# Two attention layers: the value products of two steps in one batch, and 16 buffers of exponentials instead of 8

## The reference

```python
# layer 0: 16 heads of 16, causal
scores = jnp.einsum('bhqd,bhkd->bhqk', q, k) * scale
scores = jnp.where(causal, jnp.finfo(scores.dtype).min, scores)
out = jnp.einsum('bhqk,bhkd->bhqd', jax.nn.softmax(scores, axis=-1), v)
# layer 1: 16 heads, each with two halves of 8 and one v of 16, no mask
def attend(qh, kh):
    scores = jnp.einsum('bthd,bshd->bhts', qh, kh) * SCALE
    p = jax.nn.softmax(scores, axis=-1)
    return jnp.einsum('bhts,bshe->bthe', p, v12)
a = attend(q1, k1) - lam * attend(q2, k2)     # then a norm and Wo
```

## Time and profile before

| | us |
|---|---|
| median of 3 runs | 4248.61 |
| lowest, highest | 4227.96, 4248.86 |
| profiled execution, its own time | 4232.43 |
| its span | 4230.7 |
| granted TensorE clock, mean | 0.894 |

### The profile page before, as it was taken

The page is one execution under the profiler, slowest core; times in us unless marked ns, Lnnn a source line. Parts: engine busy times, 40 slices in busy tenths (PEclk is TensorE's granted clock), DMA queues, the critical chain, the costliest instruction groups (busy, mean ns, idle before and its releaser), DMA issues. The chain is left out here.

```text
span 4230.7 us, 63916 instructions
## 1 busy us (share of the span) xinstructions
PE 3516.9 (83%) x19000; PEld 1700.2 (40%) x19000; DVE 2917.2 (69%) x4353; ACT 1941.1 (46%) x3763; POOL 766.1 (18%) x1063
## 2 busy tenths in 40 slices
PE   7599999766478885999999999999965769999758
PEld 4244444433234352333333333333333435554625
DVE  6557676346546687988888888888745457776374
ACT  2156666222111032777777777777741213334121
POOL 3222223123300051000000000000022434445000
PEclk9669999788789996999999999999987879999678
DMA  5311121000010061000000000000000231110202
GB/s 196 112 36 47 46 46 31 18 35 10 0 41 15 20 198 38 23 19 17 20 22 17 21 21 17 23 19 17 10 3 29 88 123 42 28 36 1 88 17 71
DMA packets 81131, 175.80 MB, mean 42 GB/s; under 512 B 21592, under 2 KB 39008, under 8 KB 79424
## 3 DMA queue, kind: packets, MB, share of 16 engines
q1 hardware_dynamic: 79968, 165.76, 12.9%
q10 hardware_dynamic: 864, 6.29, 0.4%
HBM read 87.76 MB, written 54.72 MB: 34 GB/s over the span
## 5 line engine op out<-in xcount | busy, mean ns | idle before, releaser
L631 DVE TENSOR_REDUCE L_attn_tops<-L_attn_psM 128x2 f32<-128x1024 f32 (+3 forms) x1408 | 1560.9, 1148 | 337.3 <-PE L_attn_psM L741 329.2
L568 ACT ACTIVATE L_attn_E<-L_attn_psS 128x512 f32<-128x512 f32 (+3 forms) x2816 | 1389.3, 575 | 583.4 <-PE L_attn_psS L700 580.0
L700 PE MATMUL L_attn_psS<-L_attn_Q,L_attn_K 64*128 64x512 f32 (+3 forms) x2816 | 995.5, 437 | 108.0 <-ACT L_attn_E L568 40.1
L741 PE MATMUL L_attn_psM<-L_attn_K,L_attn_Q 62*128 62x512 f32 (+3 forms) x2816 | 1023.6, 484 | 57.1 <-DMA L_attn_K<-parts_k 30.0
L700 PEld LDWEIGHTS L_attn_psS<-L_attn_Q,L_attn_K 64*128 64x128 f32 x2816 | 474.4, 192 | 806.1 <-ACT L_attn_E L568 634.1
L716 PE MATMUL L_attn_psO<-L_attn_E,L_attn_V 128*32 128x512 f32 (+3 forms) x5632 | 738.6, 598 | 0.0
L741 PEld LDWEIGHTS L_attn_psM<-L_attn_K,L_attn_Q 62*128 62x128 f32 x2816 | 433.9, 195 | 170.4 <-DVE L_attn_tops L631 53.0
L526 POOL TENSOR_TENSOR L_AO<-L_attn_o 128x128 f32 (+1 forms) x64 | 29.4, 459 | 1463.2 <-DVE L_attn_o L664 1463.2
L1436 PE MATMUL m_psE<-m_we,m_xT 128*128 128x512 f32 x512 | 235.1, 619 | 0.0
L535 POOL TENSOR_SCALAR_AFFINE_SELECT L_attn_E<-L_attn_E 128x128 f32<-128x128 f32 x512 | 146.6, 293 | 458.6 <-ACT L_attn_E L568 447.4
L2134 ACT ACTIVATE x_E<-x_psS 128x512 f32<-128x512 f32 x256 | 138.9, 595 | 175.3 <-PE x_psS L2257 158.0
(11 more groups left out here) (339 smaller groups left out, 3787.7 us busy)
## 6 DMA issues: line engine op xcount, KB each, us to landing
parts_q<-L_proj_parts SPq DMA_DIRECT2D x64, 256.0 KB
parts_k<-L_proj_parts SPq DMA_DIRECT2D x64, 256.0 KB
L_attn_Q<-parts_q SPq DMA_DIRECT2D x192, 64.0 KB
L_attn_K<-parts_k SPq DMA_DIRECT2D x192, 64.0 KB
L_attn_Q<-parts_q SPq DMA_DIRECT2D x64, 128.0 KB
L_attn_K<-parts_k SPq DMA_DIRECT2D x64, 128.0 KB
queries<-x1p_qo SPq DMA_DIRECT2D x16, 512.0 KB
keys<-x1p_ko SPq DMA_DIRECT2D x16, 512.0 KB
```

The source lines that it names most:

```text
L568: act.activation(E[(4 * n + s) % 8][:, c0:], psS[bank][:, c0:], ACT.Exp, scale=scale).then_inc(e_done, 1)
L631: dve.tensor_reduce(dst, src, AX, ALU.max).then_inc(m_read, 1)
L700: pe.matmul(psS[bank][:, c0:], K[g.slot][r:r + RH, c, kt * P:(kt + 1) * P], Q[g.slot][r:r + RH, c, q * HALF + c0:(q + 1) * HALF], start=Tr ...
L741: last = pe.matmul(psM[bank][:, j * HALF:j * HALF + n], Q[t.slot][r:r + TOP, c, qt * P:(qt + 1) * P], K[t.slot][r:r + TOP, c, h * HALF:h * ...
```

## The change

TensorE issues no product in odd steps. In every second step (`step % 2 == 0`, from step 2 on) it issues the products of the two steps before, one behind the other, after the four pairs of that step. The last two products of a group come together where the last one came alone, at n = LATE. E has 16 buffers (4 * RING) instead of 8, and the counts that wait for products (`o_done`) start at RING = 4 instead of 2, so that an exponential waits for the product of four steps earlier instead of two.

```diff
+    RING = 4
+    assert NS % 2 == 0 and all(e % 2 for e in ends)
...
-        E = [m.sb(f"{tag}_attn_E{k}", [P, HALF]) for k in range(8)]
+        E = [m.sb(f"{tag}_attn_E{k}", [P, HALF]) for k in range(4 * RING)]
...
-                        pool.wait_ge(o_done, (g + -2).times(NS, 2))
+                        pool.wait_ge(o_done, (g + -2).times(NS, RING))
...
-                        act.activation(E[(4 * n + s) % 8][:, c0:], psS[bank][:, c0:], ACT.Exp, scale=scale).then_inc(e_done, 1)
+                        act.activation(E[(4 * n + s) % (4 * RING)][:, c0:], psS[bank][:, c0:], ACT.Exp, scale=scale).then_inc(e_done, 1)
...
-                    act.wait_ge(o_done, g.times(NS, 2 + ends[q] + 1))
+                    act.wait_ge(o_done, g.times(NS, RING + ends[q] + 1))
...
-                pe.sem_inc(o_done, 2)
+                pe.sem_inc(o_done, RING)
...
-                        if live and step >= 1:
-                            product(g, step - 1, s_item(t, place)[0] + 3)
+                        if live and step >= 2 and step % 2 == 0:
+                            for j in (step - 2, step - 1):
+                                product(g, j, s_item(t, place)[0] + 3)
                         if old and k == 0:
-                            product(t + -2, NS - 1, s_item(t, s_place(LATE - 1, 3, last, old))[0] + 4)
+                            for j in (NS - 2, NS - 1):
+                                product(t + -2, j, s_item(t, s_place(LATE - 1, 3, last, old))[0] + 4)
```

More of the change, by code:

```diff
@@ L532, in trim @@
                         pool.wait_ge(e_done, s_item(t, place + s)[0] + 4)
-                        block = E[(4 * n + s) % 8][:, c0:c0 + P]
+                        block = E[(4 * n + s) % (4 * RING)][:, c0:c0 + P]
                         pool.sem_inc(passed, 1)
@@ L716, in product @@
                         last = pe.matmul(psO[32 * s:32 * s + 32, c0:HALF], V[g.slot][:, kt, s // shared, :],
-                                         E[(4 * n + s) % 8][:, c0:], start=(kt == 0), stop=(n == ends[q]),
+                                         E[(4 * n + s) % (4 * RING)][:, c0:], start=(kt == 0), stop=(n == ends[q]),
                                          skip_group_check=True)
```

## The result

| | before | changed |
|---|---|---|
| median, us | 4241.05 (4 runs, 4227.96 to 4248.86) | 4336.98 (4 runs, 4329.3 to 4347.01) |
| profiled execution's span | 4230.7 | 4337.7 |
| layer 0, first to last product | 561.3 | 527.3 |
| layer 1, first to last product | 1438.9 | 1569.9 |

The changed kernel is slower by a ratio of 1.0237 (95% interval 1.0214 to 1.0261). Layer 1 lost 131 us and layer 0 gained 34; about 10 of the 107 us between the spans lie outside the two layers. The forecast was 4360 us, in a range of 4300 to 4420.

What follows compares the result with a forecast made beforehand. A loop of scores and exponentials waiting for each other, closed by the product, bounds layer 1. +135 + 2 - 18 = +119 us takes 4232.4 to 4351; adding 8 for other runs gives about 4360 us, range 4300 to 4420.

Steps and rivals of the forecast that it cites:

- The loop of the earlier trace sets 2.61 us: Layer 1 before the change: scores, exponentials and product wait for each other, setting 2.61 us a step; VectorE doesn't.
- Joined products, 1.90 us: Layer 1: two joined products take 1.90 us until the next score, bounds 1.81 and 2.00.
- ScalarE's chain, 5.43: Layer 1: exponentials free the score banks so that products start at 3.53 us and end at 5.43, against 5.22 before.
- VectorE's chain, 5.77: Layer 1: the second reduction holds up a matmul ahead of the last score; products start at 3.87, period 5.77 us.
- Layer 1, +137 us: Layer 1: 245.5 two-step periods each 0.55 us longer, +135 us, and 10 periods without maxima, +2 us.
- Rival 1: Layer 1: ScalarE's chain alone closes the period at 5.43 us, +52 us there, 4276 us in all; chance 0.13.
- Rival 2: Whole kernel: no change, as layer 1's +52 us meets layer 0's -55, 4231 to 4240 us; chance 0.07.
- Rival 3: Layer 1 faster: waits of scores for exponentials disappear, period 4.56 us, -162 us, about 4078 us; chance 0.04.
- Rival 4: Products joined in the text but split by a wait, so the change doesn't do what it says; no chance given.
- Buffers and counts at nothing: Both layers: larger E and shifted product counts cost and save nothing; the rest as a whole within +-15 us.
- Layer 0, -18 us: Layer 0: 96 periods each 0.19 us shorter through TensorE's savings, -18 us, bounds -55 to +20.
- TensorE's own savings: 0.10 per joined product and 0.09 for a turn: Layer 0: joining saves 0.10 us per product and 0.09 where a turn to a product becomes one to a pair.

Runs made afterwards that it cites:

- e5: Kernel before the change, with layer 1's reductions reading half of the columns: step 2.61 us as before, layer 1 1422.4 us, 16.5 shorter.
- e6: Kernel before the change, with each product issued ahead of the step's third pair instead of behind its fourth: 4370.79 us, ratio 1.033.
- e4: Changed kernel, with layer 1's reductions reading half of the columns: period 5.43 us, layer 1 1487.5 us, 82 less than in the changed kernel.
- e3: Kernel before the change, with products joined in layer 1 only: 4372.79 us, ratio 1.0334 to before.
- e2: Kernel before the change, with 16 buffers and shifted counts but every product in its old place: 4234.8 us, ratio 0.9993.
- e9: Kernel before the change, with only products 10 and 11 of each layer 0 group joined: 4276.16 us, ratio 1.0077.
- e7: Changed kernel, with the two products issued ahead of the last pair of every second step: 4707.23 us, ratio 1.111.

## Why the prediction was right, step by step

**The loop of the earlier trace rows sets 2.61 us.** Right: VectorE with half of its work changed nothing (e5), and a moved product gave 2.67 as the same terms said (e6).

**Joined products, 1.90 us.** 2530.50 - 2528.64 = 1.86 in the changed kernel, between the taken value and the low bound 1.81.

**ScalarE's chain, 5.43.** Measured 5.43 once it was alone (e4), by two terms that were each 0.05 off in opposite directions.

**VectorE's chain, 5.77.** Measured 5.74; the products started 3.88 us after the first score (2528.64 - 2524.76), forecast 3.87. The terms of the earlier trace rows carried over. L743 was to wait for a reduction once a period; in the period shown it waits twice, ahead of the third tile too, and VectorE's four reductions still follow each other without a gap (4.62 us).

**Layer 1, +137 us.** The sum came out (+131, and +125 in e3), but its two terms didn't. Up to the last group of maxima the layer grew from 1382.4 to 1496.8 us, +114 where the 245.5 periods were to give +135: a plain period grew by 0.52 instead of 0.55, and a group at full clock by 4.05 (43.75 to 47.8), which is 0.51 for each of its eight periods. The last turns, without maxima, grew from 56.4 to 73.1 us:

```profile
3047.70:3104.10 56.40, 46.00 (x265) 13.93 (x265) 2.21 (x8) 43.29 (x85) 0.92 (x2) 1.00 0.00 1
```
```profile
3132.90:3206.00 73.10, 66.67 (x265) 20.36 (x265) 2.21 (x8) 42.36 (x85) 0.91 (x2) 0.78 0.00 1
```
```profile
3147.72 3.03 PE L718 MATMUL L_attn_psO<-L_attn_E,L_attn_V 128*32 128x512 f32 x16
```

That is +17 where the prediction has "10 periods, +2 us". It took the durations at full clock, and there the granted clock fell to 0.78: two products took 3.03 us instead of 1.92. e3 and e4, joined in layer 1 as well, show 0.82 and 0.76 in that place, and all kernels with one product a step 1.00. An error of -21 and one of +15 came near to cancelling, and that was luck.

**The rivals.** Rival 1 is refuted by e4 against the changed kernel, where halving the reductions moved the period from 5.74 to 5.43. Rival 2 is refuted by the ratio. Rival 3 is refuted by the traces of joined products in layer 1: no bank is filled while they run. Rival 4 is refuted by the row of 16 products in one train of 1.92 us.

**Buffers and counts at nothing.** Right (e2).

**Layer 0, -18 us.** It was near in size (-34, bounds -55 to +20) and wrong in kind. The step that failed is "TensorE's own savings: 0.10 per joined product and 0.09 for a turn". A group at full clock takes 32.5 us either way. What the changed kernel has less of is time at half clock, 52 us instead of 127, most of it at the start of the layer, and the prediction has no term for that. The clock stood in the earlier trace rows, 0.93 for layer 0 against 0.99 for layer 1, and was read past. The lower bound was reasoned wrongly too. Scores' waits for exponentials did halve (60.8 to 27.1 us in 250 to 700 us) and a group at full clock got no shorter; and the product's wait for trimming, which was to go, stayed (12.5 to 12.1):

```profile
PEld L_attn_psS L702 <- ACT L_attn_E L570: 27.1, 72, 1.0
...
PEld L_attn_psO L718 <- POOL L_attn_E L537: 12.1, 38, 0.4
```

**The sum.** The forecast was +119, and +107 lie between the spans. By parts it is +135, +2, -18 and nothing against +114, +17, -34 and +10 outside the layers. So the mechanism of layer 1's steps was right, and the closeness of the total is in part luck. The forecast of 4360 us stands against 4336.98: of the 23 us, 12 are the sum's, 8 are what I added for runs above the profiled one, and 2 are that the changed kernel's median lies below its own profiled run (4339.4); the rest is rounding.

## What to carry to other kernels

Where engines hand each other work through a few buffers, write down the loop with its durations, and then again with the change in it. A batch that saves fixed parts on one engine starves the others once it is longer than the stock in their buffers: here 1.90 + 0.81 us against two reductions, 2.36 us, with three score banks. Before crediting a small gain to an engine's own work, compare the same unit of work at the same granted clock, and count the time at the lower clock in both kernels. Here it was worth the whole gain of layer 0 in the changed kernel and, in the last turns of layer 1, most of a loss of 17 us that the sum put at 2.

## What the runs showed of the hardware

- In layer 0 of the kernel before, TensorE stood idle over 1 us once a group, and after some of these waits, not all, the granted clock was 0.50 for about 10 us. Which waits do it isn't settled. With waits of 25.8 instead of 16.7 us in all (e9), the mean clock from 220 to 720 us was 0.83 instead of 0.91; in e7 it was 0.82 with waits of 5.6 us.
- A group of layer 0 around such a stretch took 37.5 us instead of 32.6.
- In the last turns of layer 1 the granted clock was 1.00 with one product at a time and 0.78 with two joined; two joined products took 3.03 us there instead of 1.92.
- With four rounds of products the weight loads of the first two rounds start together (x8 at 2528.64) and those of the third 0.46 us later (x4 at 2529.10), when the second round starts: one round ahead, in the same rows of the array, while matmuls stream.
